# One VectorE product of 1120 columns in place of three of 280 columns and ten ScalarE copies per span of edges

## The reference

```python
h = relu(x @ W_ft + b_ft)
transformed = h[src] @ W_conv + b_conv
for i in range(4):                         # four "views"
    aberr = 1 / (gamma_i * (1 + v_rel_i * dir_sum))     # one number per edge and view
    agg = segment_sum(transformed * aberr, dst)         # [12500, 128] per view
    ...                                    # batch norm, relu, softmax weight
z = concat(views) @ W1 + b1 ; layer norm ; relu ; z @ W2 + b2
x = layernorm(x + that)
x = layernorm(x + second_layer(x))         # another weighted sum over the same edges
```

## Time and profile before

| | us |
|---|---|
| median of 3 runs (lowest, highest) | 5224.44 (5221.98, 5233.14) |
| profiled execution: its time | 5245.52 |
| profiled execution: span from first to last instruction | 5242.0 |
| second walk, window 1940 to 2660 | 720 |
| of it TensorE, VectorE, ScalarE, GpSimd busy | 654.28, 585.14, 412.86, 478.81 |

### The profile page before, as it was taken

How to read it: one execution, slowest core, us unless ns; L and a number is a source line. 1 busy time by engine, 2 the same in 40 slices (tenths; PEclk the granted TensorE clock), 3 DMA queues, 4 the chain that set the end, 5 groups by cost and what they waited for, 6 DMA issues and landing times. The chain is left out here.

```text
span 5242.0 us, 87816 instructions
## 1 busy us (share of the span) xinstructions
PE 3399.6 (65%) x21709; PEld 2929.8 (56%) x21710; DVE 3112.9 (59%) x9016; ACT 1517.1 (29%) x4294; POOL 3398.0 (65%) x3492
## 2 busy tenths in 40 slices
PE   3567777777777729999927865555555555555555
PEld 2355555555555528888826755555555555555554
DVE  0688888888888888888875653333333333333332
ACT  1355555555555525555513430000000000000000
POOL 1477777777777726666600017777777777777776
PEclk9788888888888869999969987777777777777777
DMA  9344444344444417887783432222222222222221
GB/s 88 104 109 107 112 108 110 106 111 108 110 108 110 109 51 201 201 202 200 204 243 115 126 103 59 59 59 59 59 59 59 59 59 59 59 59 60 59 60 51
DMA packets 538387, 535.02 MB, mean 102 GB/s; under 512 B 306734, under 2 KB 432250, under 8 KB 538328
## 3 DMA queue, kind: packets, MB, share of 16 engines
q0 software_dynamic: 111408, 227.67, 18.7%
q1 hardware_dynamic: 270918, 272.21, 17.3%
q10 hardware_dynamic: 156002, 34.46, 4.3%
HBM read 365.54 MB, written 168.49 MB: 102 GB/s over the span
## 5 line engine op out<-in xcount | busy, mean ns | idle before, releaser
L2126 POOL DMA_INDIRECT g_h_row<-h_table,g_at_dst x1666 | 1588.2, 953 | 511.0 <-issue 505.3
L2172 PE MATMUL g_ps<-g_h_row,g_same 128*128 128x129 f32 x6664 | 1210.6, 361 | 900.4 <-DMA g_h_row<-h_table,g_at_dst 900.4
L2172 PEld LDWEIGHTS g_ps<-g_h_row,g_same 128*128 128x128 f32 x6664 | 1149.0, 270 | 962.0 <-DMA g_h_row<-h_table,g_at_dst 684.1
L742 POOL DMA_INDIRECT w_src_row<-node_table,w_at_src x1099 | 1114.3, 1014 | 339.7 <-issue 276.4
L1404 PE MATMUL w_pw<-w_weighed,w_row_in 128*128 128x224 f32 x3140 | 635.1, 358 | 58.1 <-DMA w_row_in<-gathered 44.7
L1418 POOL DMA_INDIRECT w_row_in<-node_table,w_at_late x471 | 478.8, 1017 | 295.9 <-issue 158.3
L2195 DVE TENSOR_SCALAR g_code_i<-g_record 128x17 int32<-128x17 f32 x98 | 18.2, 186 | 1068.5 <-DMA g_h_row<-h_table,g_at_dst 1066.6
L1404 PEld LDWEIGHTS w_pw<-w_weighed,w_row_in 128*128 128x128 f32 x3140 | 589.7, 191 | 107.4 <-issue 101.5
L2140 ACT ACTIVATE g_ydev<-g_ydev 128x2 f32<-128x2 f32 (+2 forms) x50 | 10.1, 203 | 2102.8 <-DVE g_ydev L2244 2102.8
L2209 DVE TENSOR_SCALAR g_same<-g_iota_f,g_lo,g_record 128x256 f32<-128x256 f32 x1666 | 554.4, 409 | 100.8 <-PE g_ps L2172 100.4
L853 PE MATMUL w_pr<-ident_b,w_slots 128*56 128x128 bf16 x1570 | 164.6, 243 | 493.4 <-ACT w_apart L795 457.2
(11 more groups left out here) (252 smaller groups left out, 4329.4 us busy)
## 6 DMA issues: line engine op xcount, KB each, us to landing
gathered<-w_src_row SPq DMA_DIRECT2D x157, 462.0 KB
w_row_in<-gathered SPq DMA_DIRECT2D x157, 462.0 KB
aggT<-w_total SPq DMA_DIRECT2D x157, 224.0 KB
g_h_row<-h_table,g_at_dst POOLq DMA_INDIRECT x1666, 2.5
aggT<-w_zeros ACTq DMA_DIRECT2D x157, 159.5 KB
a_in<-aggT SPq DMA_DIRECT2D x50, 500.0 KB, 5.6
a_again<-aggT SPq DMA_DIRECT2D x24, 1024.0 KB, 6.6
w_src_row<-node_table,w_at_src POOLq DMA_INDIRECT x1099
```

The source lines that it names most:

```text
L742: pool.indirect_dma_start(src_row[q.h][:, k, :], None, node_table, bass.IndirectOffsetOnAxis(ap=at_src[q.h][:, k:k + 1], axis=0),).then_in ...
L2126: pool.indirect_dma_start(h_row[s][:, j, 0:F], None, h1_table, bass.IndirectOffsetOnAxis(ap=at_dst[s][:, j:j + 1], axis=0),).then_inc(rows ...
L2172: last = nc.tensor.matmul(ps[q.h][t][:, :], same[s][:, j, t * P:(t + 1) * P], h_row[s][:, j, :], start=(s == 0 and j == 0), stop=(s == 1 a ...
```

## The change

VectorE multiplies the one-hot by all four views at once: the one-hot is read once for each view (a repeat in the middle of its pattern), `aberr` is read with views inside tiles and each number repeated 56 times, and the result is written as 1120 columns in one stretch. ScalarE's five products per unit and their semaphore are gone; what is left to it in this walk is the copy of the late indices.

```diff
-        VECTOR_VIEWS, SCALAR_VIEWS = (0, 1, 3), (2,)
-
...
-                by_vector, by_scalar = (sem(ctx, f"w_by_{n}") for n in ("vector", "scalar"))
+                by_vector = sem(ctx, "w_by_vector")
...
                             dve.wait_ge(put_ready, u + 1)
-                            for v in VECTOR_VIEWS:
-                                last = nc.vector.tensor_tensor(
-                                    weighed[b % 4][:, :, v, :], put[b % 4][:, :, :],
-                                    aberr[:, v, here].unsqueeze(2).to_broadcast([P, TPU, WIN]),
-                                    ALU.mult)
-                            last.then_inc(by_vector, 1)
+                            nc.vector.tensor_tensor(
+                                weighed[b % 4][:, :, :, :],
+                                put[b % 4][:, :, :].unsqueeze(2).to_broadcast([P, TPU, VIEWS, WIN]),
+                                aberr[:, :, here].rearrange("p v k -> p k v").unsqueeze(3)
+                                .to_broadcast([P, TPU, VIEWS, WIN]), ALU.mult).then_inc(by_vector, 1)
...
                                 stage_late(g + AHEAD, i + (s + AHEAD) // ALL, (s + AHEAD) % ALL)
-                            act.wait_ge(put_ready, u + 1)
-                            for v in SCALAR_VIEWS:
-                                for k in range(TPU):
-                                    last = nc.scalar.activation(
-                                        weighed[b % 4][:, k, v, :], put[b % 4][:, k, :], ACT.Copy,
-                                        scale=aberr[:, v, bass.ds(u * TPU + k, 1)])
-                            last.then_inc(by_scalar, 1)
...
                             pe.wait_ge(by_vector, u + 1)
-                            pe.wait_ge(by_scalar, u + 1)
```

## The result

The changed kernel takes 5303.16 us (median of 6 runs, 5284.87 to 5308.55), the kernel before, run beside it, 5224.75 us. The ratio is 1.0143, 95% interval 1.0127 to 1.0159: 78 us slower, where no change was forecast and 5249 was the top of the range. The profiled execution, 5284.87 us with a span of 5283.2, is the shortest of the six, and the profiled one of before, 5245.52 us, lay above all six of its kernel (the longest was 5233.14), so the two traces show only half of that difference.

What follows compares the result with a forecast made beforehand. SyncE's stores, each awaiting the landing of the one before, were taken to set the pace at 4.48 us per span. VectorE's lateness added 1 us, other terms 0: 5225.5 us against the median of 5224.44, range 5215 to 5249.

Steps and rivals of the forecast that it cites:

- The product: VectorE's 1120-column product in the second walk: 1325 ns by width, 0.155 us more per unit, 49 us over the walk.
- three in a row: VectorE's three 280-column products of before overlap: 1.17 us from first start to last end, not 3 x 446 ns.
- VectorE's own span: VectorE's time per span of the second walk without waits: 4.06 us before, 4.37 after, below 4.48.
- What bounds the kernel before: Second walk: SyncE's stores each wait for the one before to land, 1.38 us in 145 of 154 spans; span 4.48 us.
- The late indices: ScalarE's index copies run ahead; GpSimd's 15.0 us of waits for them become waits for TensorE; effect 0.
- The rivals: Uneven spans make VectorE the pace (5249, 0.13); slower product (0.06); VectorE already the pace (0.05); ScalarE's absence helps (5202; faster 0.07).
- two rivals, 5273 and 5315: 5273: VectorE already sets the pace, all 49 us show, chance 0.05. 5315: product slower than its width says, 0.06.
- ScalarE: ScalarE's products go, but VectorE ends a unit 0.04 us later; 7.5 us of TensorE waits move to VectorE; no gain.
- What I named as a sign of being wrong: Product over 1.38 us, SyncE's waits naming the carry last in most spans, or TensorE awaiting weighed one-hots far over 17 times.
- VectorE's waits ahead of the carries: Sign expected in the profile after: these waits in the second walk fall from 64 us to 15 or 20.

Runs made afterwards that it cites:

- two products of 560: The changed kernel, but the product of 1120 columns in two instructions of two views (560 columns each): 5248.96 us, ratio 1.0003 to the kernel before.
- one-hot in PSUM: The changed kernel, but the one-hot lies in PSUM, so the product has one input in SBUF: 5248.51 us, ratio 0.9998 to the kernel before.

## Why the prediction was wrong

**The product** was right: 1327 ns against 1325. So was the account of three in a row, which overlap; (4.60 - 4.20) / 2 = 0.20 us per unit between four short products and one long one is what the overlap gives (0.21).

**VectorE's own span** was put too high. 4.37 us was forecast and 4.20 measured where nothing else paces. What was off is the 4.06 taken for the kernel before, not the growth: from four products back to three, at 0.365 us each, it is 4.60 - 2 x 0.365 = 3.87 us. The direction was harmless: VectorE is not the bound after the change, as the text said.

**What bounds the kernel before** is borne out: SyncE's wait for the store ahead. Two kernels with other spans of VectorE and GpSimd (two products of 560, one-hot in PSUM) keep its time, and moving the loads off SyncE's queue makes it faster by 0.26%. Why a store takes so long to land stays open.

**The step that failed** is "The late indices". It asked only when GpSimd is released and found that nobody waits for the late rows, "so this is 0". It took the length of a gather as given. The gathers grew from 1017 to 1315 ns, 3 x 0.30 = 0.90 us per span (the issue time between them shrank from 156 / 154 = 1.02 us per span to 119 / 142 = 0.84), and GpSimd's own span went from (471 + 156) / 154 = 4.07 us, with the issue time between gathers taken in

```profile
POOL w_row_in L1418 <- issue: 156.4, 415, 1.3
```

to 4.86 us, past the 4.48 of the store chain. That is 0.38 us per span and 60 us over 157. The carries of before and after (min/median/max, first and last start)

```profile
L1332 DVE TENSOR_TENSOR w_total<-w_pw,w_total x157: 624/625/626, 1949.9 to 2652.5; 128x448 f32<-128x448 f32 x157
L1330 DVE TENSOR_TENSOR w_total<-w_pw,w_total x157: 616/625/626, 1939.2 to 2697.0; 128x448 f32<-128x448 f32 x157
```

give (2697.0 - 1939.2) - (2652.5 - 1949.9) = 55 us between the two profiled executions. Their whole spans differ by 41 us, mostly because the walk of after began 11 us earlier, behind stages that the change doesn't touch. The medians differ by 78 us; of that the traces show 55 in the walk, and where the other 23 lie is not shown, since the profiled execution of after is the only one of the six below 5300 us.

**The rivals** had no case for GpSimd at all. I had worked out floors for TensorE, VectorE and SyncE and read GpSimd's 471 of 690 us as room, without the issue time between its instructions; its floor was as near the pace as VectorE's. The 5303 us measured lies between the prices of two rivals, 5273 and 5315, and bears out neither: the product took 1327 ns, and VectorE was not the pace. The signs were in the trace of before. The gather of the third walk, by its group, and the spread of it and of that of the second (min/median/max, first and last start):

```profile
L2126 POOL DMA_INDIRECT g_h_row<-h_table,g_at_dst x1666 | 1588.2, 953 | 511.0 <-issue 505.3 <-DVE g_at_dst L2197 3.6 <-PE g_ps L2172 2.1
```

```profile
L2126 POOL DMA_INDIRECT g_h_row<-h_table,g_at_dst x1666: 940/944/1230, 3127.9 to 5222.6; - x186
L1418 POOL DMA_INDIRECT w_row_in<-node_table,w_at_late x471: 938/989/1242, 1940.4 to 2635.7; - x157
```

An instruction with a median of 944 ns in one place has one of 989 in the other, and in both it can take over 1200. Its length is not its own alone: something holds it now and then, and in the second walk more often.

**ScalarE** was right: no gain from its products going. With them back in place the gathers and the span stay as they are in the changed kernel (1327 ns, 4.90 us).

**What I named as a sign of being wrong** did show, if narrowly: SyncE waits for the total in 142 of 142 spans, and in 142 - 65 = 77 of them it came last. VectorE's waits ahead of the carries, which were to fall to 15 or 20 us, are 81, since all of the walk now waits for GpSimd.

## What to carry to other kernels

Before several VectorE instructions with two inputs in SBUF become one, look at what GpSimd does meanwhile: here the gaps between short instructions were what let its gathers through. Work out the floor of every engine per turn of the loop, with the issue time between its instructions, not busy time alone, and look at the spread of each instruction that the edit doesn't touch. If one long instruction is wanted, one of its inputs in PSUM takes the hold away.

## What the runs showed of the hardware

- A gather instruction of GpSimd that starts 0.2 to 0.8 us into a VectorE product of 1120 columns with two SBUF inputs ends 0.81 to 0.83 us after the product; where nothing holds it, it takes 0.94 us. With one input in PSUM the same product holds nothing: 258 gathers that start inside one take 0.95 us on average.
- The longest gather goes by the length of one VectorE product, 0.75 to 0.80 us above it: 1242 ns with products of 280 columns (446 ns), 1514 with 560 (744), 1787 with 840 (1034), 2089 with 1120 (1327). With one input in PSUM it is 1219, 0.76 above the one-hot instruction of 463 ns. The gathers with 560, 840 and 1120 columns, and with 1120 and the one-hot in PSUM:

```profile
L1409 POOL DMA_INDIRECT w_row_in<-node_table,w_at_late x471: 938/944/1514, 1942.5 to 2649.4; - x157
L1417 POOL DMA_INDIRECT w_row_in<-node_table,w_at_late x471: 938/1066/1787, 1938.1 to 2642.9; - x157
L1407 POOL DMA_INDIRECT w_row_in<-node_table,w_at_late x471: 940/1220/2089, 1929.1 to 2690.9; - x157
L1407 POOL DMA_INDIRECT w_row_in<-node_table,w_at_late x471: 938/944/1219, 1936.6 to 2643.5; - x157
```

- The means of a gather by VectorE's products of a unit: 1003 ns (two of 560 columns), 1017 (three of 280), 1046 (four of 280), 1088 (one of 840), 1315 (one of 1120). They don't follow VectorE's load. They also depend on how many gathers start inside a product: with two of 560 it is 198 of 466, with four of 280 it is 334 of 461. What sets that share is not explained.
- In the changed kernel 316 of 456 gathers, 69%, start inside a product, though products take 378 of 690 us, 55%.
- The kernel before took 5205.94 to 5248.73 us by the median on two chips, 0.8%, more than the effects of most experiments here; in two sets on one of these chips it took 5248.73 and 5236.58.
